# Two layers of cross-attention: mask bits on two DMA queues, and the first two units' values projected one slot earlier

## The reference

```python
q = hidden_state @ Wq + bq                  # 32 heads of 16
k = encoder_hidden_state @ Wk + bk          # 8 key-value heads of 16
v = encoder_hidden_state @ Wv + bv
scores = einsum('bkgld,bksd->bkgls', q, k) * scale + mask
attn = softmax(scores, axis=-1)
out = einsum('bkgls,bksd->bkgld', attn, v) -> (b, l, 512)
x = out @ Wo + bo + hidden_state
return (x - mean) * rsqrt(var + 1e-6) * gamma + beta
```

## Time and profile before

| | us |
|---|---|
| median of 3 runs | 1731.52 |
| the three runs | 1728.42, 1732.39, 1731.52 |
| time of the profiled execution | 1728.31 |
| its span | 1726.5 |

### The profile page before, as it was taken

How to read it: one execution, slowest core, us unless ns; L and a number is a source line. 1 busy time by engine, 2 the same in 40 slices (tenths; PEclk the granted TensorE clock), 3 DMA queues, 4 the chain that set the end, 5 groups by cost and what they waited for, 6 DMA issues and landing times. The chain is left out here.

```text
span 1726.5 us, 36049 instructions
## 1 busy us (share of the span) xinstructions
PE 1695.4 (98%) x10911; PEld 1007.9 (58%) x10911; DVE 1266.7 (73%) x1713; ACT 1041.5 (60%) x2370; POOL 572.2 (33%) x1169
## 2 busy tenths in 40 slices
PE   7999999999999999999999999999999999999997
PEld 4556556566556565565665565665665655656652
DVE  5578777777777787776787776777776877767776
ACT  2566666665666566665656665666665666656564
POOL 3133333233333333332333332333323333323332
PEclk9999999999999999999999999999999999999999
DMA  7656555546545555546565455455454455454541
GB/s 242 160 150 151 145 145 122 143 120 155 148 121 143 135 131 146 151 116 156 147 169 149 127 123 134 112 140 147 106 133 130 121 139 141 108 136 114 141 114 55
DMA packets 288534, 235.83 MB, mean 137 GB/s; under 512 B 140874, under 2 KB 262980, under 8 KB 288356
## 3 DMA queue, kind: packets, MB, share of 16 engines
q1 hardware_dynamic: 267524, 205.82, 45.6%
q10 hardware_dynamic: 20960, 29.38, 7.3%
HBM read 101.39 MB, written 22.02 MB: 71 GB/s over the span
## 5 line engine op out<-in xcount | busy, mean ns | idle before, releaser
L940 DVE TENSOR_REDUCE mx<-ms 128x2 f32<-128x750 f32 x896 | 809.4, 925 | 397.2 <-PE ms L1112 391.2
L765 ACT ACTIVATE probs<-sc 125x448 f32<-125x448 f32 x1522 | 744.0, 542 | 280.0 <-PE sc L1083 276.0
L1112 PE MATMUL ms<-ks,qs 96*128 96x375 bf16 (+1 forms) x2560 | 437.9, 324 | 12.4 <-DVE mx L940 9.3
L1083 PE MATMUL sc<-qs,ks 99*125 99x448 bf16 x1522 | 427.0, 357 | 1.8 <-ACT probs L765 1.5
L1133 PE MATMUL pv<-probs,vs 125*32 125x448 f32 x3048 | 312.8, 543 | 0.0
L1083 PEld LDWEIGHTS sc<-qs,ks 99*125 99x125 bf16 x1522 | 192.5, 136 | 198.4 <-ACT probs L765 126.2
L1112 PEld LDWEIGHTS ms<-ks,qs 96*128 96x128 bf16 (+1 forms) x2560 | 174.0, 98 | 190.8 <-issue 66.5
L1190 PE MATMUL job<-wo,on 128*112 128x512 f32 x504 | 257.3, 592 | 0.0
L956 DVE RECIPROCAL orec<-osum 128x112 f32<-128x112 f32 x256 | 213.2, 835 | 4.2 <-DMA osum<-oraw 4.2
L1208 PE MATMUL job<-xT,wq 128*128 128x224 f32 x1008 | 214.3, 356 | 1.3 <-DMA xT<-in_xT 1.3
L1208 PEld LDWEIGHTS job<-xT,wq 128*128 128x128 f32 x1008 | 187.1, 190 | 20.9 <-ACT qf L807 7.1
(11 more groups left out here) (72 smaller groups left out, 1053.6 us busy)
## 6 DMA issues: line engine op xcount, KB each, us to landing
ctxT<-in_ctxT SPq DMA_DIRECT2D x64, 750.0 KB, 4.9
qs<-qp SPq DMA_DIRECT2D x756, 56.0 KB, 2.5
ks<-kp SPq DMA_DIRECT2D x768, 46.9 KB, 3.0
osum<-oraw ACTq DMA_DIRECT2D x125, 112.0 KB, 2.9
oc<-oraw ACTq DMA_DIRECT2D x125, 112.0 KB, 4.0
mask<-in_mask SPq DMA_DIRECT2D x64, 164.1 KB, 5.6
xT<-in_xT SPq DMA_DIRECT2D x32, 224.0 KB, 4.8
xin<-in_x SPq DMA_DIRECT2D x32, 224.0 KB, 3.1
```

Of the source, the lines that this page charges most:

```text
L765: nc.scalar.activation(probs[0:KCS, k, j, :], bank[0:KCS, 0:GL], ACT.Exp)\
L940: nc.vector.tensor_reduce(mx[o][:, cols], ms[n % 2][:, :, 0:S2], AX_X, ALU.max).then_inc(max_done[o], 1)
L1083: last = nc.tensor.matmul(bank[0:KCS, 0:GL], ks[p][0:KM, g, rows], qs[p][0:KM, g, :], start=True, stop=not masked)
L1112: last = nc.tensor.matmul(to, qs[o][0:KT, group, cols], ks[o][0:KT, group, :], start=True, stop=not masked)
```

## The change

The mask's pieces 0 to 2 stay on SP's queue (`BSYNC = 3`), pieces 3 to 6 are issued by ACT after it has cast the keys' rests. `wv` and `bv` move ahead of the mask's pieces on SP. The query sends of half 0 (second and third parts) move from ACT to SP, ahead of the last ks DMAs of half 1. The values of unit (0, 0) are projected at the end of PE's opening slot, before the dummy matmuls, of which there are 8 (in 16 passes) and no longer 12; DVE takes them between the sixth and the seventh piece of the mask. The values of unit (1, 0) take the place in slot (1, -1) that those of unit (0, 0) had, and slot (0, 0) projects none. The keys of unit (1, 0) go to pieces 3 to 6, and ACT casts their rests in piece 7, right behind the maxima rows. In layer 1's loads one DMA is added and each load after the first comes one slot later.

```diff
+BSYNC = 3
-CLOCK = (3, 12)
+CLOCK = (3, 8)
-KEYS_AT = [..., {0: (0,), 1: (1,), 2: (2,), 3: (3,)}]
+KEYS_AT = [..., {3: (0,), 4: (1,), 5: (2,), 6: (3,)}]
-        NK, NQ, NV, NW, NR = 2, 2, 2, (3, 7), (2, 5)
+        NK, NQ, NV, NW, NR = 2, 2, 2, (3, 8), (2, 5)
...
                     sp.wait_ge(q_p1[0], 2)
                     stack_terms(0, 0, qs[0], qp, 0, of=(0,))
+                    sp.wait_ge(q_p2[0], 2)
+                    stack_terms(0, 0, qs[0], qp, 0, of=(1,))
+                    sp.wait_ge(q_p3[0], 2)
+                    stack_terms(0, 0, qs[0], qp, 0, of=(2,))
                     stack_terms(0, 1, ks[0], kp[0], 1, of=(0,))
                     load_ctx(1, 0, 0)
-                    load_wv(0, w_v)
                     stack_terms(0, 1, qs[0], qp, 0, of=(0,))
                     load_mask(0, 0, 0)
...
                 if (p, i) == (0, PER - 2):
-                    load_wq(1, w_in[1], slice(2, DC))
+                    load_wq(1, w_in[1], slice(2, 3))
                 if (p, i) == (1, PER - 2):
+                    load_wq(1, w_in[1], slice(3, DC))
+                if (p, i) == (0, PER - 1):
                     load_wo(1, rows_in[1], slice(0, 2))
-                if (p, i) == (0, PER - 1):
+                if (p, i) == (1, PER - 1):
                     load_wo(1, rows_in[1], slice(2, NG))
-                if (p, i) == (1, PER - 1):
+                if (p, i) == (0, PER):
                     for dst, key in ((bo, "bo"), (gamma, "gamma"), (beta, "beta")):
...
             load_xT(1, 0, 0)
-            for n in range(BLOADS):
+            load_wv(0, w_v)
+            for n in range(BSYNC):
                 sp.dma_start(mbits[:, BROW * n:BROW * (n + 1)], mbits_d[n]).then_inc(mf_in[n], 16)
...
                     query_rests()
                     query_parts()
-                    key_rests()
                     max_parts(o, 0, ahead, None)
-                    key_lasts()
+                    key_parts()
...
                     k_out()
                     cast_keys()
+                    for n in range(BSYNC, BLOADS):
+                        act.dma_start(mbits[:, BROW * n:BROW * (n + 1)], mbits_d[n]).then_inc(mf_in[n], 16)
...
-                    send(0, qs[0], qp, 0, (1,))
-                    send(0, qs[0], qp, 0, (2,))
                     send(1, qs[0], qp, 0, (1, 2))
...
+                    if opens(p, i) and k == COLUMNS_AT[q][0]:
+                        cast_keys()
...
+            def take_values(u, n, layer):
+                dve.wait_ge(v_ps[u], n + 1)
+                nc.vector.tensor_tensor(vs[u] ..., job ..., bv[layer] ..., ALU.add).then_inc(v_ready[u], 1)
             for n in range(BLOADS):
                 dve.wait_ge(mf_in[n], 16)
                 nc.vector.tensor_reduce(...)
+                if n == BLOADS - 2:
+                    dve.wait_ge(w_v, 16 * NV)
+                    take_values(0, 0, 0)
...
+                    if opens(p, i) and p == 0:
+                        pe.wait_ge(w_v, 16 * NV)
+                        project_values(range(KC), p, proj, lay[3])
```

More of the change, by code:

```diff
@@ L66 @@
 NSTACK = 2 * NT
-CLOCK = (3, 12)
+CLOCK = (3, 8)
 LATE_HEADS_AT = [{}, {0: (2,), 1: (3,)}]
 HEADS_AT = [{10: (0,), 11: (1,)}, {8: (0,), 9: (1,), 10: (2,), 11: (3,)}]
-KEYS_AT = [{2: (0,), 3: (1, 2), 4: (3,)}, {2: (0, 1), 3: (2, 3)}, {0: (0,), 1: (1,), 2: (2,), 3: (3,)}]
+KEYS_AT = [{2: (0,), 3: (1, 2), 4: (3,)}, {2: (0, 1), 3: (2, 3)}, {3: (0,), 4: (1,), 5: (2,), 6: (3,)}]
 VALUES_AT = [{1: (0, 1), 2: (2,)}, {4: (0,), 5: (1,), 6: (2,)}, {8: (0,), 9: (1,), 10: (2,)}]
@@ L867, in slot @@
                         outputs(o, 1, post)
-                    if k == KEYS_END[q] + 1 and j_ok:
+                    if k == KEYS_END[q] + 1 and j_ok and not opens(p, i):
                         cast_keys()
@@ L917, in _ @@
             nc.vector.tensor_scalar(bqs[0][:, :], bq[0][:, :], SCALE, None, ALU.mult).then_inc(consts, 1)
+            def take_values(u, n, layer):
+                dve.wait_ge(v_ps[u], n + 1)
+                nc.vector.tensor_tensor(
+                    vs[u][:, :, :, :, 0], job[0:KCS, 0:KC * P].rearrange("p (c g d) -> p c g d", c=KC, d=HD),
+                    bv[layer][:, :].rearrange("p (g d) -> p g d", d=HD).unsqueeze(1)
+                    .to_broadcast([KCS, KC, NKV, HD]), ALU.add).then_inc(v_ready[u], 1)
             for n in range(BLOADS):
@@ L932, in slot @@
                 q = table_row(p, i)
+                values_here = a_ok and not (isinstance(i, int) and (p, i) == (0, 0))
                 if starts_layer(p, i):
@@ L942, in values @@
                 def values():
-                    if first_values(p, i):
-                        dve.wait_ge(w_v, 16 * NV)
-                    dve.wait_ge(v_ps[o], ahead + 1)
                     if p_ok:
                         dve.wait_ge(pv_ps[o], 2 * (post + 1))
[L948 to L951, removed]
+                    if opens(p, i):
+                        take_values(p, proj, lay[3])
+                    else:
+                        take_values(o, ahead, lay[1])
                 def reciprocal(n):
@@ L1029, in slot @@
                             deviation()
-                        if k == max(VALUES_AT[q]) and step == 0 and a_ok:
+                        if k == max(VALUES_AT[q]) and step == 0 and values_here:
                             values()
@@ L1058, in slot @@
                     job_free = [(o_evac[p], stored + 1) if s_ok else (mt_evac[p], 2 * main + 1) if m_ok else None]
-                    if isinstance(i, int) and (p, i) == (0, 0):
-                        job_free[0] = (v_ready[p], 1)
+                    values_here = a_ok and not (isinstance(i, int) and (p, i) == (0, 0))
+                    if isinstance(i, int) and (p, i) in ((1, -1), (0, 0)):
+                        job_free[0] = (v_ready[1 - p], 1)
                     def take_job_bank():
@@ L1147, in max_columns, with project_values @@
                             job_free[0] = (mt_evac[u], 2 * n + h + 1)
-                    def project_values(chunks):
+                    def project_values(chunks, u, n, layer):
                         if 0 in chunks:
                             take_job_bank()
-                        if 0 in chunks and first_values(p, i):
-                            pe.wait_ge(w_v, 16 * NV)
                         for c in chunks:
                             for t in range(DC):
-                                last = nc.tensor.matmul(job[0:KCS, P * c:P * c + P], ctxT[o][:, t, KCS * c:KCS * c + KCS],
-                                                        wv[lay[1]][:, t, :], start=(t == 0), stop=(t == DC - 1))
+                                last = nc.tensor.matmul(job[0:KCS, P * c:P * c + P], ctxT[u][:, t, KCS * c:KCS * c + KCS],
+                                                        wv[layer][:, t, :], start=(t == 0), stop=(t == DC - 1))
                         if KC - 1 in chunks:
-                            last.then_inc(v_ps[o], 1)
-                            job_free[0] = (v_ready[o], ahead + 1)
+                            last.then_inc(v_ps[u], 1)
+                            job_free[0] = (v_ready[u], n + 1)
                     def project_keys(chunks):
@@ L1263, in slot @@
                             max_columns(p, 1, main)
-                        if k in VALUES_AT[q] and a_ok:
-                            project_values(VALUES_AT[q][k])
+                        if k in VALUES_AT[q] and values_here:
+                            project_values(VALUES_AT[q][k], *((p, proj, lay[3]) if opens(p, i) else (o, ahead, lay[1])))
                         if k in QUERIES_AT[p] and j_ok:
```

## The result

The changed kernel takes 1738.14 us in the median of 7 runs (1735.65 to 1738.93), the kernel before 1730.41 us on the same chip (7 runs, 1727.70 to 1732.53): ratio 1.0044, 95% interval 1.0032 to 1.0055. It is slower, by 7.7 us, and lies outside the forecast range of 1726.5 to 1736.5 us. Its profiled execution took 1737.99 us with a span of 1736.2, 9.7 more than the one of before.

What follows compares the result with a forecast made beforehand. PE, busy 98% of the span, bounds the steady slots; only the first 75 us could move much. +0.5 and -0.4 make +0.1 on 1731.5, written as 1731.7 us; likeliest 1729 to 1734, 8 in 10 1726.5 to 1736.5.

Steps and rivals of the forecast that it cites:

- wv and bv are 256 and 62.5 KB, 0.33 MB; at 410 GB/s 0.8 us: Opening: loads moved ahead of the mask's pieces delay them only by their bytes, 0.8 us.
- SP's chain: Slot (0, 0): SP's nearly unbroken DMA issues for the ks stack, from 43.57 us, forecast to start 1.0 us later.
- Service in order of issue over both queues: Opening: DMA engines serve both queues by issue time, so ACT's last mask piece lands 1.3 us later, at 26.2.
- fourth rival: Opening: queues share fairly, bits and stacks alternate, flag near 31.7, first maxima 33.3 or later; 1733.9 us, chance 0.12.
- fifth rival: Slot (0, 0): without values the clock falls again, up to 3.3 us, partly hidden; 1734 to 1736 us, chance 0.20.
- keys' context wait: Opening: PE's 2.0 us wait for unit (1, 0)'s context, until 32.82, was forecast to go.
- removed 3.05 us of values: Slot (0, 0): PE loses 3.05 us of value projection, yet the slot was forecast at net +0.5 us.
- -0.4: Change of layer: PE's 0.90 us DMA wait at 815 us may shrink, taken as half.
- a second queue adds no bandwidth: Opening: with the DMA engines full, a second queue can change only the order of loads.
- +0.1 us: Whole kernel: net effect forecast, +0.5 from slot (0, 0) and -0.4 from the change of layer.
- half clock: Opening: after the dummies PE idles and its clock falls from 2.4 to 1.2 GHz, about 30.7 to 37.3 us before.

Runs made afterwards that it cites:

- a_wv_early: The kernel before with the loads of wv and bv moved ahead of the mask's pieces, nothing else: ratio 1.0036, 1737.20 us.
- c_one_wv_mid: The changed kernel with bv behind unit (1, 0)'s context, all mask pieces on SP, half 0's sends on ACT, wv behind the third piece: 1.0007, 1730.64 us.
- a_two_queues: The kernel before with mask pieces 3 to 6 on ACT's queue and half 0's query sends on SP's, nothing else: ratio 0.9996, 1730.30 us.
- c_bv_apart: The changed kernel with bv on its own semaphore behind unit (1, 0)'s context and DVE's take of the values moved later: ratio 1.0007, 1731.35 us.
- f_start: The kernel before with 6 passes of dummy matmuls added at the head of slot (1, -1): ratio 0.9998.

## Why the prediction was wrong

**The step that failed** is "wv and bv are 256 and 62.5 KB, 0.33 MB; at 410 GB/s 0.8 us". It counted bytes. wv behaved so (0.6 us for 256 KB). bv, a fifth of the bytes, cost 4.9 us alone, and the two together 6.9 (a_wv_early). The last piece was forecast to be reduced at 26.4 and was at 33.85. The flag was forecast 1.5 us late and came 9.0 late; the first maxima 31.4 and came at 37.74; SP's chain 44.6 and came at 50.64. Everything later hangs on this. The trace of before could not show it: there bv is issued at 25.9, behind all pieces of the mask. The bound for a load that had never stood there should have been wide; the range had no term for it. With bv and the second queue taken out (c_one_wv_mid, which also has wv behind the third piece and the sends of half 0 back on ACT) the steps come out near the forecast, in one profile: last reduction 26.46 (26.4), flag ready 29.19 (29.2), first maxima 31.52 (31.4), SP's chain 45.16 (44.6).

**"Service in order of issue over both queues"** was wrong too. Counts by queue in the changed kernel from 21 to 22 us, which answer to the earlier trace rows:

```profile
DMA packets 110, 0.31 MB, mean 314 GB/s; under 512 B 21, under 2 KB 63, under 8 KB 110
## 3 DMA queue, kind: packets, MB, share of 16 engines
q10 hardware_dynamic: 55, 0.27, 81.6%
q1 hardware_dynamic: 55, 0.04, 16.7%
```

As many packets from one queue as from the other, large ones of the mask beside small ones of the stacks; from 16 to 27 us they are 604 and 633, with 3.02 and 0.78 MB. This agrees with the turns that the Trainium skill, DMA: Bandwidth & Descriptors, section Queues, rings and completion order, describes, and which the prediction had as its fourth rival. The trace of before held it too, a few us behind the rows that I had read: from 27 to 28 us q1 has 141 packets and q10 140. q10 begins at 16 us though its first issue was at 13.16, and I had taken such an empty start for an order. It is likely the same in the earlier trace rows, where q10 had nothing for 3 us behind the first ACT send. The rival's mechanism occurred, but in a_two_queues it cost nothing in the time (0.9996). Its profile has the last piece at 28.50, the first maxima at 32.45, SP's chain at 45.61 and the first `pv<-probs` at 69.30, each 2 to 3.6 us later than in the profile of before; as that profile is of a fast execution, this is no more than shifts of kernels that lose nothing. Where the late bits are absorbed isn't shown.

**The fifth rival's mechanism**, the second fall of the clock in slot (0, 0), happened in every profile of a kernel that takes the values out of this slot without filling it, and in none of those that leave them in. It costs about 1.5 us by one pair of profiles, less than half of the 3.3 us that the prediction had as its upper end: it eats what the missing values would give, and is hardly a loss on top.

**What was right.** The keys' context wait of 2.04 us is gone, in c_one_wv_mid too, where the maxima start only 1.8 us later than before. The removed 3.05 us of values bring nothing by themselves, since the maxima wait for the `ks` stack (1.09 us there). The steady slots and the change of layer are unchanged; PE's context wait before layer 1 is 0.88 us instead of 0.90, so the -0.4 for it didn't come. The engines being full, a second queue adds no bandwidth: from 10 to 28 us a_two_queues moved 6.10 MB, the kernel before 6.47. Without bv the change is worth what the prediction gave for all of it: 1.0007, between 0.9998 and 1.0016, against a forecast of +0.1 us. In part that is luck: in the profile of c_bv_apart the flag was ready at 32.89 instead of 29.2, the first maxima came at 33.94 instead of 31.4 and SP's chain at 46.66 instead of 44.6, and the time didn't follow.

**Two small slips of the prediction.** The half clock began at about 30.5 and not 30.7: 0.73 as the mean of 30 to 31 us gives that. And the fourth rival's 2 us more than the forecast of 1731.7 make 1733.7, not 1733.9. Neither changes the argument.

**Still open.** How the one row's price grows and why reading it is slow; which engines fall behind; how much of the loss is the half clock from 31 to 45 us. The two loads together cost 1.4 us more than the sum of each, which the intervals don't tell from nothing.

## What to carry to other kernels

Price a load by how it is dealt out and what it reads, not by its bytes alone: here a small vector spread from one DRAM row over 125 partitions held up everything queued behind it, so put such loads behind the last large load that somebody waits for, or move them alone and measure. When work is taken out of a slot in which PE waits for something else, look whether what is left keeps the clock up; here three matmuls into a free bank kept it. And follow one recurring instruction through both traces before explaining anything: a constant distance says at once in which microseconds the change acts.

## What the runs showed of the hardware

- bv, 62.5 KB from one row of 512 bytes to 125 partitions, put ahead of 5.25 MB of loads, cost 4.9 us; 64 KB from 128 different rows cost 0.0004 of the time (0.7 us; 1.6 by the medians), inside the interval.
- A load to 127 partitions ahead of them made the first large piece 3.0 us later than one to 128, in one profile each; the time rose by 0.0010 against 0.0004, with intervals that overlap.
- With bv in front, 0.55 MB of what was queued behind the first large piece had moved before that piece was complete; with 128 different rows in front, 0.03 MB.
- A second queue that starts behind a full first one moved nothing for about 3 us (issued at 13.16, first packets from 16), and then, from 16 to 27 us, about as many packets as the first (604 and 633).
- From the flag in SBUF to PE's first matmul behind the branch on it, 1.06 us pass in f_start, and 1.06 in the changed kernel.
- Near 1695 us the clock fell in the profiles of some kernels that are equally fast and not in that of before; the same 24 matmuls take 2.46 us at 2.4 GHz and 4.71 at 1.2 GHz.
